# First attention layer: where the last two value products and the division of a batch stand in the next batch's round

## The reference, cut to what matters

```python
xn = layernorm(x)
s = attention0(xn)                 # softmax(q k^T / sqrt(8) + relative bias) v, then w_out
g = silu(mixture_of_experts(xn))   # 8 experts, top 2 of each token
x = x + s * g
xn = layernorm(x)
s = attention1(xn)                 # causal, with gains on the attention, the identity and a running mean
g = silu(xn @ W.T + b + (xn @ V_r) @ C.T)
x = x + s * g
```

## Time and profile before

| what | value |
|---|---|
| runs | 1212.32, 1213.5, 1210.34 us |
| profiled execution: span from first to last instruction | 1206.2 us (its own time is not listed apart) |
| median of the runs less that span | 6.1 us |
| TensorE matmul busy | 922.8 us (76%) |
| VectorE busy | 735.9 us (61%) |
| ScalarE busy | 455.4 us (38%) |
| GpSimd busy | 383.3 us (32%) |
| mean granted TensorE clock | 0.906 |
| attention of layer 0, rounds 2 to 17 | about 141 to 512 us of the span |

### The profile page before, as it was taken

The page is one execution under the profiler, slowest core; times in us unless marked ns, Lnnn a source line. Parts: engine busy times, 40 slices in busy tenths (PEclk is TensorE's granted clock), DMA queues, the critical chain, the costliest instruction groups (busy, mean ns, idle before and its releaser), DMA issues. The chain is left out here.

```text
span 1206.2 us, 22735 instructions
## 1 busy us (share of the span) xinstructions
PE 922.8 (76%) x7845; PEld 555.7 (46%) x7846; DVE 735.9 (61%) x1156; ACT 455.4 (38%) x800; POOL 383.3 (32%) x370
## 2 busy tenths in 40 slices
PE   1865869898899999789999804467778788778786
PEld 0723435454554454345555503344445555455553
DVE  6644859898999899746556539244334544344452
ACT  1250434444444444433434315423333334333332
POOL 6027731000110010047677745102232222332213
PEclk9987989999999999989999955678988989889899
DMA  4874321221122111312122131122221122221110
GB/s 117 224 132 114 89 69 43 56 60 52 42 57 60 50 42 42 108 45 57 53 56 55 45 111 35 38 58 57 59 53 48 46 59 62 60 49 46 46 47 16
DMA packets 81031, 77.06 MB, mean 64 GB/s; under 512 B 11141, under 2 KB 72905, under 8 KB 77817
## 3 DMA queue, kind: packets, MB, share of 16 engines
q1 hardware_dynamic: 72284, 65.39, 22.2%
q0 software_dynamic: 4352, 8.99, 2.5%
q10 hardware_dynamic: 4352, 2.10, 0.6%
HBM read 46.35 MB, written 29.32 MB: 63 GB/s over the span
## 5 line engine op out<-in xcount | busy, mean ns | idle before, releaser
L1135 DVE TENSOR_REDUCE mx<-ps 128x4 f32<-128x1024 f32 (+1 forms) x224 | 270.3, 1218 | 234.3 <-PE ps L1349 182.7
L1279 ACT ACTIVATE probs<-probs 128x1024 f32<-128x1024 f32 x128 | 135.3, 1057 | 171.7 <-DVE probs L1145 169.3
L1398 PE MATMUL ps<-probs,vpad 128*32 128x256 f32 (+1 forms) x2048 | 141.3, 365 | 19.6 <-ACT probs L1279 19.4
L1145 DVE TENSOR_TENSOR probs<-ps,tabB 128x1024 f32<-128x1024 f32 x128 | 152.8, 1215 | 3.7 <-PE ps L1369 3.7
L1284 ACT ACTIVATE probs<-ps 128x1024 f32<-128x1024 f32 x96 | 98.2, 1024 | 140.9 <-PE ps L1375 124.9
L1089 POOL TENSOR_TENSOR qkr<-qkf,qk 128x512 f32<-128x512 f32 x28 | 32.4, 1157 | 331.4 <-ACT qk L1246 331.4
L1102 POOL TENSOR_TENSOR probs<-probs 128x512 f32<-128x512 f32 x64 | 78.8, 1263 | 170.0 <-PE ps L1398 170.0
L1341 PE MATMUL ps<-tabA,eyeb 128*128 128x512 bf16 x256 | 100.3, 392 | 34.8 <-DMA qs<-zrow 25.2
L1347 PE MATMUL ps<-maskA,eyeb 128*128 128x256 bf16 x128 | 43.0, 336 | 80.9 <-DMA qs<-zrow 80.9
L1343 PE MATMUL ps<-ks,qs 128*128 128x256 bf16 x512 | 100.0, 278 | 0.0
L1155 DVE RECIPROCAL rden<-ps 128x256 f32<-128x256 f32 x32 | 56.0, 1751 | 54.6 <-PE ps L1398 36.5
(11 more groups left out here) (225 smaller groups left out, 1664.6 us busy)
## 6 DMA issues: line engine op xcount, KB each, us to landing
parts_d<-qk SPq DMA_DIRECT2D x32, 384.0 KB, 2.8
qs<-parts_d SPq DMA_DIRECT2D x32, 192.0 KB
ks<-parts_d SPq DMA_DIRECT2D x32, 192.0 KB
slots_in<-probs SPq DMA_DIRECT2D x1, 4680.0 KB
probs<-slots_in SPq DMA_DIRECT2D x72, 65.0 KB, 1.8
qs<-parts_d SPq DMA_DIRECT2D x32, 128.0 KB
ks<-parts_d SPq DMA_DIRECT2D x32, 128.0 KB
probs<-mixed SPq DMA_DIRECT2D x16, 256.0 KB, 3.3
```

What stands on the lines that cost most here:

```text
L1135: nc.vector.tensor_reduce(mx[:, s.buf(), t, heads[0]:heads[-1] + 1], ring[:, slot].rearrange("p (h n) -> p h n", n=w), AX.X, ALU.max).then ...
L1145: nc.vector.tensor_tensor(probs[:, j, :].rearrange("p (h n) -> p h n", n=T), ring[:, slot].rearrange("p (h n) -> p h n", n=T), v.tabB[:, h ...
L1279: nc.scalar.activation(probs[:, j, :], probs[:, j, :], ACT.Exp).then_inc(exp_done, 1)
L1398: mm = nc.tensor.matmul(od[32 * q:32 * q + 32, T * what + t0:T * what + T], lhs, probs[:, j, w * n:w * n + w], start=(j == 0 and what == 0 ...
```

## The change

TensorE, in layer 0: the value products of units 6 and 7 of batch k-2 move from the start of the round to position 3, behind A0, the projection, A1 and A2, and ahead of B0. VectorE, in layer 0: `divide` moves from the start of the round to position 3, behind the maxima of A0 to A2 and ahead of the bias addition of B0. Layer 1 keeps its order. In rounds 16 and 17, which have no first-pass units, nothing stands between the start of the round and position 3.

```diff
@@ vector: body @@
-                if layer == 0 and s.has(-2):
-                    divide(s)
                 for pos, (kind, j) in enumerate(U.order):
+                    if layer == 0 and pos == 3 and s.has(-2):
+                        divide(s)
                     if U.exists(s.k, kind):
                         (maximum if kind == "A" else add_bias if layer == 0 else lambda *a: None)(s, j, U.slot(s.k, pos))
@@ tensor: body @@
-                if s.has(-2):
+                if layer and s.has(-2):
                     values(s, -2, NU - 2)
                     values(s, -2, NU - 1)
                 if s.k == 0:
                     projections(s)
                 for pos, (kind, j) in enumerate(U.order):
+                    if layer == 0 and pos == 3 and s.has(-2):
+                        values(s, -2, NU - 2)
+                        values(s, -2, NU - 1)
                     if pos == 1 and s.has(1) and s.k != 0:
                         projections(s)
```

## The result

| | before | after |
|---|---|---|
| median of four runs | 1211.33 us (1209.17 to 1213.5) | 1264.04 us (1251.62 to 1269.11) |
| ratio, 95% interval | | 1.044 [1.0399, 1.0481], slower |
| profiled execution: time, span | span 1206.2 us | 1269.11 us, span 1267.3 us |
| TensorE matmul busy, mean granted clock | 922.8 us, 0.906 | 949.4 us, 0.882 |
| VectorE busy | 735.9 us | 738.5 us |

A forecast was written before the change was run, and what follows sets the result against it. The prediction took a first-layer loop through the stack transfer, about even with VectorE's work, as the bound; +29.0 us for the longer loop and +21.6 for low clock made +50.6 on 1212.3, so 1263 us, range 1238 to 1276.

The forecast's parts named there:

- The ring: First-layer loop: A0, add0 (B0's bias addition), exponential, parts, store, loads, next A0; turn 23.80 to 26.5 us, +29.0 in all.
- first half: From A0 to add0 (bias addition of B0), at full clock: 7.8 us where 5.09 stood.
- second half: From add0 (bias addition of B0) through exponential, parts, store and loads to the next A0: 18.71 us, unchanged.
- 1.8 us extra on round 4: Round 4's way from add0 to the next A0 took 20.50 instead of 18.71 us before; added once.
- The low clock: TensorE idles 2.56 us before A0, so its clock falls each round: 1.8 us times 12, 21.6 us.
- The cover of round 2: VectorE's 8.10 us wait for the scatter of sorted rows in round 2 hides the 2.7 us of later work.
- estimate of round 3: Stack long landed; TensorE's units, value products and division put add0 at 182.5 instead of 182.92, a gain of 0.4 us.
- The clock did not hold: Judges the first rival: same loop in layer 0, TensorE's clock stays high, 1241 us; chance 0.17.
- third rival: Low clock lasts through most of A0 to V7 in many rounds: 3 to 5.7 us each, 1277 to 1310; chance 0.14.
- The landing was the limit: Forecast that A0 waits for the stack's loads, 11.84 us from first issue to A0; under 9.2 us would refute it.
- second rival: Stack loads land early, A0 follows the transpose directly, 0.06 us a round: 1213 us, not slower; chance 0.05.
- The signs: New profile: stack wait about 30 us, rounds 6 to 15 at 27 to 29 us, clock 0.5 behind A0.

The follow-up runs named there:

- e5: Changed kernel with eleven unused TensorE matmuls run while it would wait for the stack: 1292.14 against 1260.95 us for the kernel before, ratio 1.0266.
- e11: Changed kernel repeated without an edit, on the chip of the repeated filled-wait run: 1310.34 us, 1.043 of the kernel before.
- e3: Changed kernel with ScalarE's second stack part (parts_two) ahead of the exponential of B0 in layer 0: 1266.52 against 1260.95 us, 1.0055 of the kernel before.
- e1: Changed kernel with value products V6 and V7 back at the round's start, only the division late: 1291.73 against 1260.95 us, 1.0239 of the kernel before.
- e9: Kernel before with ScalarE's second stack part (parts_two) ahead of the exponential, in the second layer only: 1200.83 against 1257.09 us, ratio 0.9567.
- e0: Changed kernel repeated without an edit, on a chip without the stall: 1262.48 against 1209.25 us for the kernel before, ratio 1.0439.
- e4: Kernel before with ScalarE's second stack part (parts_two) ahead of the exponential of B0 in layer 0: 1255.89 us, ratio 0.9996.
- e2: Changed kernel with the division back at the round's start, only the value products late: 1306.41 against 1209.25 us, 1.080 of the kernel before, single execution.
- e6: e4's order plus earlier transpose and projection, A0 ahead of the value products of units 5 to 7, division behind A0's maximum: 1196.89 us, 0.9908 of kernel before.
- e7: As e6, but unit 7's products one position later and the division behind A1's maximum: 1199.0 us, 0.9906 of the kernel before.

## Why the prediction was right, and where it was off

- **The ring holds.** Its first half at full clock was put at 7.8 us; e5 has 7.7, the rounds of e11 with a clock of 1.00 7.7 to 7.8. Its second half was put at 18.71 unchanged; over rounds 4 to 14 it is 207.4 us in all, where the sum had 207.6. The sum put 1.8 us extra on round 4 alone; that round has 0.5 extra (19.23 us), and the rest is spread over the others. That the exponential carries the delay into the stack was argued from ScalarE's order alone; e3 shows it, by taking only that link out.
- **The low clock** was put at 1.8 us a round, from the one row alike. A0 to add0 is 8.5 to 10.6 us in rounds 4 to 15, in the mean 9.66, so 1.9 over 7.8: 0.7 to 2.0 in eight rounds, 2.5 to 2.8 in four. (Round 15 has no projection left, and takes 6.85 instead of 7.7 in e5, so its 7.8 was about 0.9 too much.) Together, A0 of round 4 (206.01) to add0 of round 15 (529.23) last 323.2 us, where the prediction's terms give 301.2 + 21.6 = 322.8. Before, it was 271.8: +51.4 of the span's +61.1. How much of it falls due differs between runs (e11's four rounds without), and this may be a part of the changed kernel's spread of 17 us between runs; that was not traced.
- **The cover of round 2 held only in part.** The prediction had the scatter's wait hide round 2's 2.7 us. Round 2 was at low clock too: 10.42 us from A0 to add0 instead of 6.11. And the wait ended at 170.25 instead of 166.53:

```profile
170.25 0.42 DVE L1195 TENSOR_TENSOR rows<-ps,bo 128x256 f32<-128x256 f32 x1 [5.16 <-DMA slots_in<-rows,place]
...
176.83 0.34 PE L1466 MATMUL ps<-eyeb,m 128*96 128x128 bf16 x1
...
185.99 1.21 DVE L1145 TENSOR_TENSOR probs<-ps,tabB 128x1024 f32<-128x1024 f32 x1
```

  Its last scatter was issued 1.1 us later than before, but the wait for it ended 3.7 us later; why it took longer is not settled. Round 3's add0 is at 185.99, 3.1 us later than before, where a gain of 0.4 was predicted. The estimate of round 3 itself, 9.4 us from the transpose to add0, fits the measured 9.16; it started late. With its slower second half, A0 of round 4 is 4.5 us late.
- **After the ring** the stages up to the end take 5.2 us more, which the prediction had at nothing. They do not lie in the second attention, which takes 436.5 us instead of 436.9, from its first projection (L1415, at 830.84 and 769.27) to the end. They lie ahead of it: 1.8 us up to the last exponential of the first layer (L1279, at 565.22 and 507.47), and about 4 us in the middle stage, where TensorE's mean clock from 776.40 to 830.84 is 0.50, and 0.56 in the answering stretch before (718.30 to 769.27). The change leaves that stage as it was; whether the clock alone makes the 4 us was not tested.
- **What is luck.** The span grew by 61.1 us where the sum had 50.6, since 4.5 + 5.2 us stood outside the ring. The medians differ by only 52.7 us. An execution takes 1.8 us more than its span in every run listed for the change, so the profiled one of before took about 1208.0 us (an estimate), 3 us below its median, and that of the change lies 5 us above its own. The scatter between executions is thus nearly as large as what the sum left out, and that 1263 was met this closely is partly luck.
- **The rivals.** The clock did not hold in any of the 12 rounds of the profiled execution, and not at its worst either, 5.7 us a round. But the third rival's picture, a low clock through most of the way to V7, does appear in four of them, at 2.5 to 2.8 us each, just below the 3 us that it was priced at. The landing was the limit: TensorE waits for it in all 12 rounds. Only when the ring is broken, in e3, does the second rival's picture appear, at 1.0055.
- **The signs** named came: wait for the stack 33.3 us (about 30 was said), turns of 27.9 to 29.5 (27 to 29), the reciprocal 6.96 us behind A0 (5.7 or more), 0.50 behind A0. One was off: VectorE idles 4.69 us before the first maximum, not 3.7, since A0 itself runs at half speed: the maximum starts 1.92 us behind A0's start, and 1.08 in e1, where the clock is 1.00.

## What to carry to other kernels

Before a unit is pulled into another engine's idle time, ask whether its own input is there; here it came 2.4 to 3.8 us too late, and the work that was moved away had filled just that stop. Then follow what is delayed along each in-order engine: the instruction that is late may be nobody's bottleneck, and the one queued behind it may feed the next turn of a loop. Such a link is cheap to cut (three lines on ScalarE), and worth looking for wherever the same pipeline is used again: in the second layer it was 4.3%.

## What the runs showed of the hardware that was not expected

- **A stop can move, and the clock with it.** In e1 it is 2.73 us in the middle of the round, with a clock of 0.61 in the 3 us behind it and 1.00 at A0; in e9, where the waits for the stack are shorter, the mean clock of the whole second attention is 0.94 instead of 0.88. The length of the stop alone does not decide: in e11 the clock held after one stop of 2.00 us and fell after another of 2.00, and in e3 it fell (0.55 from 201.09 to 203.09) after one of 1.02 us, ahead of which TensorE had idled 1.36 us. What decides was not found.
- **A stall of the first rounds that went with the chip, not with the kernel.** On two of the three chips of the experiments all traced kernels stand still before the ring, with several engines idle at once and the idle time put down to no work that the profile shows ("issue", "remote"). The longest such wait is 35 to 43 us. The changed kernel is among them: e0 takes 1262.48 us on one chip, e11 1310.34 on another. Waits of e4, 90 to 230 us:

```profile
ACT vpad L1262 <- remote: 42.6, 1, 42.6
...
PE ps L1343 <- issue: 39.7, 3, 22.6
```

  In the traces of e0, e2, e6 and e7, and in those of before and after, no row put down to "issue" or "remote" in the same stretch has a wait of over 8 us. The cause was not looked into.
